# Copied rows, 25 instead of 27 rounds a group, longer load rows and a store semaphore per group in the first layer of a four-layer convolution kernel

## The reference, cut to what matters

```python
def _denoise_block(x, w1, b1, w2, b2, w3, b3, a, b, c):
    trip = _triplets(x)              # channel t with its neighbours t-1 and t+1
    B, T, C, H, W = trip.shape
    xf = trip.reshape(B * T, C, H, W)
    o = a * _conv_reflect(xf, w1, b1, 1, 2) + b * _conv_reflect(xf, w2, b2, 2, 4) \
        + c * _conv_reflect(xf, w3, b3, 4, 8)          # 5x5, dilation 1, 2, 4
    return jnp.tanh(o).reshape(B, T, H, W)
y = _denoise_block(x, blk1 ...)
z = _denoise_block(y, blk2 ...)
return z                             # x = x + z, on _gn(x) as input
```

## Time and profile before

| | us |
|---|---|
| median of 3 runs | 5300.8 (5299.0 to 5303.9) |
| profiled execution, its own time | 5308.6 |
| its span, first to last instruction | 5306.8 |
| PE busy | 4988.3 (94%) |
| DVE busy | 3369.1 (63%) |
| ACT busy | 2400.5 (45%) |
| POOL busy | 1366.5 (26%) |
| queue of SP's DMAs, share of 16 engines | 68.7% |

### The profile page before, as it was taken

The page is one execution under the profiler, slowest core; times in us unless marked ns, Lnnn a source line. Parts: engine busy times, 40 slices in busy tenths (PEclk is TensorE's granted clock), DMA queues, the critical chain, the costliest instruction groups (busy, mean ns, idle before and its releaser), DMA issues. The chain is left out here.

```text
span 5306.8 us, 178754 instructions
## 1 busy us (share of the span) xinstructions
PE 4988.3 (94%) x78653; PEld 2961.4 (56%) x78653; DVE 3369.1 (63%) x6195; ACT 2400.5 (45%) x2999; POOL 1366.5 (26%) x1629
## 2 busy tenths in 40 slices
PE   4999999999999999999999988998777899999998
PEld 2444444444444467777777763433655466666665
DVE  5653453453433555555555547887999688888888
ACT  2222231231221111111111118875999699999997
POOL 0000000000002111111111100001777255555556
PEclk9999999999999999999999999999999999999999
DMA  8777777777766667667676659997887365666554
GB/s 247 241 250 232 236 252 228 237 251 231 233 206 221 206 207 233 209 206 233 207 224 216 207 161 320 326 320 247 307 309 292 120 152 149 152 152 152 150 152 120
DMA packets 366866, 1166.79 MB, mean 220 GB/s; under 512 B 60458, under 2 KB 61097, under 8 KB 287019
## 3 DMA queue, kind: packets, MB, share of 16 engines
q1 hardware_dynamic: 363928, 1152.98, 68.7%
q10 hardware_dynamic: 2162, 2.39, 0.2%
HBM read 683.58 MB, written 453.51 MB: 214 GB/s over the span
## 5 line engine op out<-in xcount | busy, mean ns | idle before, releaser
L682 PE MATMUL c_p<-c_w,wc 128*32 128x512 f16 x55296 | 3017.4, 380 | 25.5 <-DMA c_w<-xs 23.6
L682 PEld LDWEIGHTS c_p<-c_w,wc 128*32 128x32 f16 x55296 | 1761.9, 97 | 1252.5 <-issue 30.4
L742 ACT ACTIVATE c_t<-c_p,cbias,cscale 128x512 f32<-128x512 f32 x512 | 398.4, 778 | 2385.8 <-PE c_p L682 2385.7
L607 DVE TENSOR_TENSOR a_x<-c_t,a_x 128x512 f32<-128x512 f32 x256 | 222.1, 868 | 656.9 <-ACT c_t L742 656.9
L597 DVE TENSOR_SCALAR c_y<-c_t 128x512 f16<-128x512 f32 x256 | 109.4, 427 | 704.1 <-ACT c_t L742 586.9
L1705 PE MATMUL f_P<-f_qh,f_wt 64*64 64x512 f16 x4608 | 545.7, 378 | 1.8 <-DVE f_t L1601 1.8
L1705 PE MATMUL f_P<-f_hl,f_wt 64*64 64x512 f16 x4608 | 545.3, 379 | 0.0
L1866 POOL TENSOR_TENSOR f_y<-f_y,f_x 128x512 f32<-128x512 f32 x256 | 331.1, 1293 | 448.0 <-DVE f_hl L1580 442.0
L1601 DVE SCALAR_TENSOR_TENSOR f_t<-f_P,f_kk,f_ci 128x256 f32<-128x256 f32 x1024 | 423.6, 476 | 11.9 <-PE f_P L1705 7.2
L813 POOL COPY c_y<-c_y 128x16 f16<-128x16 f16 x512 | 87.2, 200 | 1278.0 <-DVE c_y L599 1278.0
L1465 POOL TENSOR_TENSOR e_hl<-e_g,e_hl 128x2048 f16<-128x2048 f32 x63 | 257.2, 4083 | 609.5 <-ACT e_hl L1415 609.5
(11 more groups left out here) (263 smaller groups left out, 5896.5 us busy)
## 6 DMA issues: line engine op xcount, KB each, us to landing
c_w<-xs SPq DMA_DIRECT2D x576, 264.0 KB, 7.8
c_w<-ys SPq DMA_DIRECT2D x576, 264.0 KB, 3.9
d_x<-x SPq DMA_DIRECT2D x128, 1024.0 KB, 7.6
x<-d_x SPq DMA_DIRECT2D x128, 1024.0 KB, 5.1
ys<-c_y SPq DMA_DIRECT2D x576, 132.0 KB
xs<-a_hl SPq DMA_DIRECT2D x70, 1056.0 KB, 11.3
a_x<-in_x SPq DMA_DIRECT2D x256, 256.0 KB, 5.6
a_x<-in_x SPq DMA_DIRECT2D x128, 512.0 KB, 5.0
```

Source lines behind the costliest of these rows:

```text
L607: v.tensor_tensor(xw[:, g, :], tl[:, :], xw[:, g, :], ALU.add).then_inc(c_lo, 1)
L682: t = p.matmul(pg[32 * j:32 * j + 32, :], wu[:, blk, wl, var, di, :], buf[:, bk, xl * PW + PAD + dx:xl * PW + PAD + dx + NW], start=(di == ...
L742: s.activation(tt_[n % 3][:, :], pp[:, n % 4, :], ACT.Tanh, bias=cbias[:, blk:blk + 1], scale=cscale[:, blk:blk + 1]).then_inc(c_act, 1)
```

## The change

- **PE:** offsets -8, -4, 0, 4, 8 keep their three rounds (15); for -2, -1, 1, 2 the low-weight round stays (4), and the high weight meets high and low rows in six rounds over two new tiles. `near` (`c_n`) holds the high plane of the 96 rows in use and, on the last 32 partitions, a copy of the low plane of a third of them; `twice` (`c_2`) holds the low plane of the other 64 partitions twice, the second time shifted by three columns, so that one round takes two offsets. 15 + 4 + 4 + 2 = 25 rounds.
- **DVE** copies three of the four pieces of the next group (`copies(n + 1)`), **ACT** the fourth, before the rest of a step. The high plane of the output moves from DVE to ACT (`high`).
- **Order of rows in the window:** `slot` puts them so that a load is four transfers of 32, 16, 8 and 8 partitions, each a plain run of eight row blocks; a load covers two groups and is issued at odd g.
- **Stores** signal one semaphore per group and buffer, and `high` waits for the same group of unit u - 2 only.
- **Set-up:** POOL makes the extra weights `wn` with twelve small copies; the swapped copy of the weights grows from 3456 to 4608 columns.

```diff
@@ def slot(row, chan) @@
-        h8, s = ((1, 0), (0, 0), (1, 1), (0, 1))[row // 8 + 1]
-        v8 = row + 8 * h8 - 16 * s
-        return 8 * (2 * v8 + chan % 2) + 4 * s + 2 * h8 + chan // 2
+        place = row + (36, 20, 0, 0, 0, 0, 4, 4)[row // 4 + 2]
+        return 4 * place + 2 * (chan % 2) + chan // 2
@@
+        near = [sb(ctx, f"c_n{i}", [128, 4, PW], F16) for i in range(2)]
+        twice = [sb(ctx, f"c_2{i}", [128, 4, PW], F16) for i in range(2)]
@@
+        def rows_in(e, n):
+            u, g = divmod(n, 4)
+            e.wait_ge(c_ld[u % 2][g // 2], n_win(u))
+            if n >= 2:
+                e.wait_ge(c_pe, n - 1)
+            return win[u % 2][:, 4 * g:4 * g + 4]
@@ DVE @@
-                def halves(u, g):
+                def low(u, g):
...
-                    v.wait_ge(c_act, n + 1)
-                    if u >= 2 and g == 0:
-                        v.wait_ge(c_yd[u % 2], n_ys(u))
...
-                    v.tensor_scalar(hi, tl[:, :], YS, None, ALU.mult).then_inc(c_hi, 1)
                     v.wait_ge(c_hi, n + 1)
                     v.scalar_tensor_tensor(lo, tl[:, :], YS, hi, ALU.mult, ALU.subtract).then_inc(c_lo, 1)
+                def copies(n):
+                    w = rows_in(v, n)
+                    v.tensor_copy(near[n % 2][0:96], w[0:96, :, 0:PW]).then_inc(c_nh, 1)
+                    v.tensor_copy(near[n % 2][96:128], w[64:96, :, PW:RW]).then_inc(c_nl, 1)
+                    v.tensor_copy(twice[n % 2][0:64], w[0:64, :, PW:RW]).then_inc(c_2a, 1)
@@ PE, products @@
-                    for di, dx in enumerate(DX):
-                        for z, (wl, xl) in enumerate(((0, 0), (0, 1), (1, 0))):
-                            for j in range(4):
...
+                    for di in (4, 0, 1, 7, 8):
+                        for wl, xl in ((0, 0), (0, 1), (1, 0)):
+                            four(wu[:, blk, wl, :, di], rows4, xl * PW + PAD + DX[di], start=(di, wl, xl) == (4, 0, 0))
...
+                    for di in (2, 3, 5, 6):
+                        four(wu[:, blk, 1, :, di], rows4, PAD + DX[di])
...
+                    p.wait_ge(c_nh, n_copied(n))
+                    p.wait_ge(c_nl, n_copied(n))
+                    for e, di in enumerate((2, 3, 5, 6)):
+                        four(wnear[:, :, e], near[n % 2], PAD + DX[di])
+                    p.wait_ge(c_2a, n_copied(n))
+                    p.wait_ge(c_2b, n_copied(n))
+                    four(wnear[:, :, 4], twice[n % 2], PAD - 2)
+                    t = four(wnear[:, :, 5], twice[n % 2], PAD - 1, stop=True)
                     t.then_inc(c_pe, 1)
@@ ACT @@
+                def high(u, g):
+                    n = 4 * u + g
+                    s.wait_ge(c_act, n + 1)
+                    if u >= 2:
+                        s.wait_ge(c_yd[u % 2][g], n_ys(u))
...
+                    s.activation(yt[u % 2][:, g, 0, PAD:PAD + NW], tt_[n % 3][:, :], ACT.Copy, scale=YS).then_inc(c_hi, 1)
+                def copies(n):
+                    w = rows_in(s, n)
+                    s.activation(twice[n % 2][64:128, :, PAD - 2:PAD - 1 + NW], w[0:64, :, PW + PAD + 1:PW + PAD + 2 + NW], ACT.Copy).then_inc(c_2b, 1)
@@ SP, load @@
-                        e.wait_ge(c_pe, 4 * (u - 2) + g + 1)
+                        e.wait_ge(c_pe, 4 * (u - 2) + g + 2)
...
-                        for h8 in range(2):
-                            e.dma_start(win[half][gp % 2 + 2 * h8:128:4, 4 * g:4 * g + 4].rearrange("p k w -> p (k w)"),
-                                        dram(src, pair(b, gp, 0, 16 * half + 4 * g) + h8 * (8 * VP - RW),
-                                             [[CP, 16], [RW, 2], [1, 4 * RW]])).then_inc(c_ld[half][g], 16)
+                        at = pair(b, gp, 0, 16 * half + 4 * g)
+                        for first, count, off in ((0, 32, 0), (80, 16, RW), (64, 8, 12 * VP - RW), (112, 8, 8 * VP - RW)):
+                            e.dma_start(win[half][first + gp % 2:first + 2 * count:2, 4 * g:4 * g + 8].rearrange("p k w -> p (k w)"),
+                                        dram(src, at + off, [[CP, count], [1, 8 * RW]])).then_inc(c_ld[half][g // 2], 16)
@@ SP, main loop @@
-                        if u + 2 < 2 * NU and not late:
-                            load(u + 2, g)
+                        if u + 2 < 2 * NU and not late and g % 2:
+                            load(u + 2, g - 1)
```

More of the change, by code:

```diff
@@ L381, in n_ys, with doubled, n_copied @@
         def n_ys(u):
-            return 16 * sum(8 + 4 * (place(r)[2] in (0, 7)) for r in range(u % 2, u, 2))
+            return 16 * sum(2 + (place(r)[2] in (0, 7)) for r in range(u % 2, u, 2))
         def n_win(u):
-            return 32 * sum(1 + (place(r)[2] == 0) for r in range(u % 2, u + 1, 2))
+            return 64 * sum(1 + (place(r)[2] == 0) for r in range(u % 2, u + 1, 2))
+        def doubled(n):
+            return 0 <= n < 8 * NU
+        def n_copied(n):
+            return n + 1
+        def rows_in(e, n):
[4 more added lines that the diff above has]
+            return win[u % 2][:, 4 * g:4 * g + 4]
         def table_of(u):
@@ L637, in _ @@
                 v0(2), v1(2)
+                copies(0)
                 for u in range(2 * NU):
@@ L651, in _ @@
                             table(table_of(u), g // 2)
-                        (total if blk else halves)(u, g)
+                        (total if blk else low)(u, g)
                         if blk:
@@ L676, in products, with four @@
                         p.wait_ge(c_act, n - 3)
-                    for di, dx in enumerate(DX):
-                        for z, (wl, xl) in enumerate(((0, 0), (0, 1), (1, 0))):
-                            for j in range(4):
-                                bk = 4 * g + j
-                                var = 0 if (half, bk) == (0, 0) else (2 if (half, bk) == (1, 15) else 1)
-                                t = p.matmul(
-                                    pg[32 * j:32 * j + 32, :], wu[:, blk, wl, var, di, :],
-                                    buf[:, bk, xl * PW + PAD + dx:xl * PW + PAD + dx + NW],
-                                    start=(di == 0 and z == 0), stop=(di == 8 and z == 2), tile_position=(0, 32 * j))
[L686 to L689, removed]
-                            if s == 1:
-                                p1_(i)
+                    def four(weights, source, at, start=False, stop=False):
+                        for j in range(4):
+                            bk = 4 * g + j
+                            var = 0 if (half, bk) == (0, 0) else (2 if (half, bk) == (1, 15) else 1)
+                            t = p.matmul(pg[32 * j:32 * j + 32, :], weights[:, var], source[:, j, at:at + NW],
+                                         start=start, stop=stop, tile_position=(0, 32 * j))
+                        return t
@@ L771, in _ @@
                         evict(u, g)
+                        if u < NU:
+                            high(u, g)
                         if st_ == 2:
@@ L841, in load @@
                         r = 16 * b + 2 * min(7, p + 1) + 2
-                        e.wait_ge(c_yd[0], n_ys(r))
-                        e.wait_ge(c_yd[1], n_ys(r + 1))
+                        for gg in range(4):
+                            e.wait_ge(c_yd[0][gg], n_ys(r))
+                            e.wait_ge(c_yd[1][gg], n_ys(r + 1))
                     else:
```

52 lines of the change are left out of this document (39 added, 13 removed).

## The result

The changed kernel takes **5450.4 us** (median; 5447.5 to 5460.9), the one before, timed beside it, takes 5301.4: ratio **1.0284, 95% interval 1.0271 to 1.0297**. It is slower by 150 us where 25 less were forecast, and lies outside the range.

A forecast was written before the change was run, and what follows sets the result against it. Before the change, block 1 was taken as bound by PE and four store-carrying DMA engines together, block 2 by PE. Block 2's -87 and block 1's +62 summed to -25 us, giving 5276 us, range 5150 to 5410.

The forecast's parts named there:

- same bytes: Block 1 loads: bytes and issues unchanged, so only rows per full engine grow, 5 for 4, adding 0.41 us a group.
- +62: Block 1, first half of the first layer: becomes DMA-bound at about 6.2 us a group, 62 us slower in all.
- Spread: Block 1 loads: eight-row transfers use eight engines including the stores' four, five long rows there for four, +89 us.
- Rival 3: Block 1 loads: rows landing in half the partitions cost half again, total 5470 us, 5328 at half that price; chance 0.13.
- The 18 us: Block 1: stores may fall further behind, up to 27 us, before PE starves, moving work later: 18 us less.
- the 12 us: Block 1, last 28 groups: they run at 5.40 us each, 12 us less.
- Rival 2: Block 1: PE's clock drops after waits for pairs of loads, 100 us over the forecast, 5376 us; chance 0.16.
- The term -87: Block 2, second half of the first layer: DVE becomes the bound at about 5.5 us a group, 87 us less.
- Waits for stores: Block 1: DVE's 110.5 us stall for stores goes, but gives nothing by itself while four DMA engines bound.
- ACT: Fourth copy and high half on ACT: 3.3 us a group in block 1, 2.7 in block 2, hidden under PE's 5.4.
- Copies: Three DVE copies a group at 0.69 us each, 2.0 us a group; about 0.9 more where they meet POOL's table products.
- rival 4: DVE copies at the slow rate put block 2 at 7.2 us a group, total about 5690 us; chance 0.06.

The follow-up runs named there:

- b_merge: Kernel before the change, with each pair of ys stores merged into four 32-row transfers of outermost count 16: 5320 us, ratio 1.0034.
- b_pool2: Kernel before the change, with each ys store cut into four transfers of 16 rows, half issued by GpSimd: 5374 us, ratio 1.0139.
- b_spread: Kernel before the change, old places and short rows, but load transfers of 32, 16, 8 and 8 rows: 5390 us, ratio 1.0166.
- b_place: Kernel before the change, with the change's row places and counts of 32, 16, 8 and 8, rows still of one group: 5475 us, ratio 1.0321.
- a_actq: Changed kernel, with its ys stores unchanged in shape but issued by ScalarE one group later: 5684 us, ratio 1.0719 to the kernel before.
- a_merge: Changed kernel, with each pair of ys stores made into four 32-row transfers of outermost count 16, issued by SP: 5251 us, ratio 0.9897.
- a_merge_v0: Same as a_merge, with VectorE's statistics step moved ahead of the copies: 5253 us, ratio 0.9907 to the kernel before.
- after: The kernel with the whole change, compared with the kernel before it: 5450 us, ratio 1.0284.
- a_merge_pool: Same as a_merge, with the merged stores issued by GpSimd instead of SP: 5256 us, ratio 0.9901 to the kernel before.
- a_pool2: Changed kernel, with each ys store cut into four transfers of 16 rows, half issued by GpSimd: 5274 us, ratio 0.9940 to the kernel before.
- a_poolq: Changed kernel, with its ys stores unchanged in shape but issued by GpSimd instead of SP: 5279 us, ratio 0.9950 to the kernel before.

## Why the prediction was wrong

**The step that failed: "same bytes".** The load part of the four engines was costed by rows alone, 5 for 4 at an unchanged time a row: 1.65 x 1.25 = 2.06 us. The rows took 1.04 us, not 2 x 0.415: 5 x 1.04/2 = 2.6 us a group, 0.54 more, and in the forecast's own form 0.54/1.16 x 228 = +106. The x rows of the neighbours became slower as well, 0.106 to 0.135: 8 x 128 rows in seven groups on 16 engines are 9.1 a group and engine, 9.1 x 0.029 = 0.27 us, /1.16 x 228 = +52. With the forecast's +62 (start included) that makes +220, where +207 was measured (202 and a start of 5). The mechanism, block 1 of the changed kernel bound by the engines that carry the stores, was right; the term was mis-sized by the price of a row. The reading of the kernel before was not borne out: had these four engines bound its block 1 together with PE, b_merge and b_pool2 should have lost the border waits, and both became slower.

**Spread.** +89 for the counts of 8: b_spread measured +88, but with twice the issues, so that the agreement may be luck in part. **Rival 3**, the price of the new places, was given 0.13 and had half of the error: +82 of 174 us by b_place. Its x1.5 was too much, x1.25 (0.83 to 1.04) is what came, places and length together. The 5328 that the prediction gives for half of the price halves the spread's part too; with x1.25 its own form gives (1.65 x 1.25 x 1.25 - 1.65)/1.16 = 0.80 us on 228 groups and 5369, and with the +52 of the x rows 5421. The Trainium skill, SBUF — State Buffer, "Door 1: The DMA port swizzle", speaks of ports reached by halves of the partitions; rows and places agree in direction (b_place; store rows confined to 32 partitions 0.107 to 0.114 us for 0.090, though 0.103 over all partitions in a_actq), but no run separates a port from another cause. The 18 us that a longer delay was to give cannot be read by themselves; the last 28 groups took 5.63 us each, not the 5.40 that the 12 us stood on.

**Rival 2.** The clock fell (0.93) after waits, 71 us of 1200. I read it as a consequence and not as a cost on top, since two rounds less changed block 1 by 14 us only, so PE's speed did not set its time. No run takes the clock alone.

**Block 2.** 5.4 to 5.6 us a group with DVE over 90% busy: 5.47 in its last 240 groups, at 96%; the copies 2.33 us against 2.0 and 0.9 in every fourth. The excess is in the first copy alone, 0.912 us in the mean from 2000 to 2900 us and 0.712 in block 1: of its 165 runs in block 2 the 51 that overlap an instruction of GpSimd took 1.42 us, the other 114 0.69, as the prediction expected of copies that meet POOL's table products. The term -87 missed the start: loads of two groups wait for stores of ys there (PE stood 20.0 us for loads from ys between 1850 and 2000 us), and the first 16 groups take 6.82 us each, +23. In a_merge, without these waits, block 2 gives -93.

**Waits for stores** went as forecast; no run takes their semaphores alone, but with the rounds and the copies they gave 14 us in block 1. **Copies**: 0.71 and 0.91 us, rival 4 false. **ACT** was nearly hidden: PE waited 9.4 us for its copy. Not foreseen: statistics steps behind the copies in DVE's order, 54 us of PE's waits; moving them ahead (a_merge_v0) gave nothing.

## What to carry to other kernels

Cost a reshaped transfer in time of an engine and not in bytes: count rows per engine, and give each row a price of its own, with a range, when its places or its length change. Where the DMA share reads 0.77 and the issuer never waits, as here, look for transfers with a small outermost count: in after the few engines that carry them set the time, and less work on TensorE gave next to nothing until they were relieved. When a relieved wait brings no time, look at what is waited for instead: in a_merge_pool it was PE's own instructions. A cut of compute can then be worth its price only together with that: after alone loses 2.8%, with merged stores it gains 1.0% (1.3% with GpSimd's issues and short rows as well), and the merged stores alone lose 0.3%.

## What the runs showed of the hardware

Rows of 16,896 bytes took 0.857 us over all 128 partitions and 1.044 where each transfer lies in half of them or less; x rows that nobody had changed went from 0.106 to 0.131 beside them. An issue took about 0.6 us on SP whatever the transfer, unless it was held: two took 7.20 us on ScalarE's queue, which then stood as SP had. On GpSimd it took 0.54 us in the mean for stores of 16 rows (a_pool2, 1152 issues), 0.50 in most cases for 32 rows (a_merge_pool) and 0.62 for 64 (a_poolq). Stores issued by GpSimd moved in rows of 4,224 bytes where the same transfer from SP moved in 2,112 (a_poolq against after). PE stood for its own instructions for 105 of 1200 us in a_merge_pool, where the DMA share was 0.90, and for 2 in a_merge at 0.92.
